# A graph kernel whose attention stage splits its weighted rows into bf16 parts in PSUM, on ScalarE and VectorE

## The chip, the cores and the metric

The kernel runs on one core of one Trainium2 chip. The metric is the device time of the whole kernel in microseconds, one launch from start to end.

## The reference

Four kinds of graph layer act on 6,250 nodes of 48 features, in eight layers, each with a residual and a norm. The change touches the second kind. With 206,250 sorted edges it weights the rows of the target node by the edge's softmax weight and sums them at the source node:

```python
seg_max = jax.ops.segment_max(logits, dst, num_segments=N)
ex = jnp.exp(logits - seg_max[dst])
...
seg_sum = jax.ops.segment_sum(ex, dst, num_segments=N)
```

In the kernel the edges stand in cells (a bucket of 128 source nodes by a bucket of 128 target nodes). A row is fetched by a one-hot matmul, multiplied by its edge's weight, and added at its node by another one-hot matmul. The fp32 rows go through TensorE exactly enough as three bf16 parts: the high part, the high part of what it leaves, and the rest.

## The kernel before

Between about 3000 and 5850 us of the span three kinds of work are interleaved over the places of one loop, `for q in range(PLACES)`. Every engine runs the same loop and takes its part of each place in the order in which the code stands; semaphores tie them together.

- **The gates** of a later layer, one quad of four edge tiles in each of the first 403 places: TensorE `hidden` (L1285, L1286), ScalarE `gates` (L1534, L1535, L1540, L1543), TensorE `gate` (L1295), VectorE `near_gates` (L2350, L2351), which runs one place later, then GpSimd's four indirect scatters (L925), here called the burst of that quad. SyncE loads the edge attributes.
- **The attention steps**, 273 groups of nine tiles (n), each in the place that `STEP_AT` names. 175 steps stand in the place right behind the step before, 78 skip one place, 20 skip two and 3 skip three. TensorE's `attend_take(n)` fetches the rows by 27 matmuls (L1377) into PSUM bank n % 2. VectorE's `attend_rows(n)` reduces (L2619) and multiplies the bank by the weights (L2626) into the fp32 buffer `row_part(n, 0)` in SBUF. In step n VectorE's `attend_step` first subtracts for group n-1 (L2634) and for group n-2 (L2638), two fp32 subtractions in SBUF; then come `attend_rows(n)`, `build_K` (L2599), `build_S` (L2589) and at times `collect`. `attend_give(n-3)` adds the rows by nine matmuls (L1406); its operand `uppers` picks every second bf16 of the fp32 buffer, which is the upper half of each number.
- **The counting of the cells**, three rounds in each step: `count_cells` on TensorE (L1418) into bank 5, `blocks_out` on ScalarE (L1633) out of it, and the next round only after that. Between the three L1633 ScalarE prepares the one-hot rows of step n+2 (`distance` L1603, `turn` L1613).

The buffers `part_slots` (four, in `meta_b`, `ring` and `VQ`) hold the split rows. The 25 last groups (`BEHIND`) have their subtractions on GpSimd behind its scatters; the change leaves them alone. Before the change `attend_take(n)` waits until the multiplication of group n-2 has read the bank (`s_msg`).

A step's row on TensorE is: take, count round 1, `hidden`, count round 2, `gate`, count round 3, give. In the profile `ps` is any PSUM bank, and `remote` as a releaser means a wait for which the profile names no work of this core.

## Time and profile before

| | us |
|---|---|
| median of 3 runs | 6898.89 |
| range of the runs | 6873.34 to 6902.73 |
| the profiled execution, device time | 6892.13 |
| its span | 6890.3 |
| TensorE busy | 3922.0 (57%) |
| VectorE busy | 4075.6 (59%) |
| ScalarE busy | 2567.7 (37%) |
| GpSimd busy | 3960.8 (57%) |

The busy times are over the whole span, whose stages have different limits; no engine is full overall. The stage with the attention steps takes over 40% of the span, and only there do instructions change. Times in the rows are in us from the span's start, and the mean of one instruction is in ns.

### The profile page before, as it was taken

The page shows a single profiled execution, that of the slowest core. Times are in us where ns is not written, and L with a number is a line of the kernel's source. Part 1 is how long each engine was busy: PE and PEld are TensorE (multiplying, and loading weights), DVE is VectorE, ACT ScalarE, POOL GpSimd, SP SyncE. Part 2 cuts the span into 40 slices and gives each one's busy share as a digit, 9 for nine tenths or more (in the row PEclk, how much of TensorE's full clock was granted, in tenths as well). Part 3 has the DMA queues.
Part 4 walks back from the last instruction along what each step waited for, and adds up shares of the span by engine and source line. Part 5 has one row for each costly group of instructions (what it writes and reads, how often), then busy time and mean ns, then how long its engine had stood idle before and what let it go on. Part 6 is the DMA issues. An engine that isn't in the chain of part 4 may idle for free.

```text
span 6890.3 us, 121918 instructions
## 1 busy us (share of the span) xinstructions
PE 3922.0 (57%) x46612; PEld 3008.3 (44%) x46613; DVE 4075.6 (59%) x7184; ACT 2567.7 (37%) x5259; POOL 3960.8 (57%) x3993
## 2 busy tenths in 40 slices
PE   5445555555555554345555555555555555887875
PEld 5344444323323333134444444444444444776774
DVE  4444443555555556345666666566666558667999
ACT  1111111111111111244455455445445445776664
POOL 2566666666666666655555555555555553225996
PEclk8555555555555555555555555555555556999998
DMA  3444311121111121123333233333333332667886
GB/s 127 167 160 161 124 49 47 48 55 49 47 49 47 48 49 47 32 50 54 58 56 57 56 58 55 56 56 58 55 58 56 55 56 54 189 189 172 193 191 130
DMA packets 1414672, 571.31 MB, mean 83 GB/s; under 512 B 1069539, under 2 KB 1353711, under 8 KB 1413953
## 3 DMA queue, kind: packets, MB, share of 16 engines
q1 hardware_dynamic: 1309185, 452.39, 29.3%
q0 software_dynamic: 104896, 110.96, 6.7%
q8 instruction: 381, 6.24, 0.4%
q14 instruction: 210, 1.72, 0.1%
HBM read 394.81 MB, written 168.16 MB: 82 GB/s over the span
## 4 chain that ended last, share of the span: by engine, by line
another core or an unknown queue 22%; PE 19%; issue 18%; ACT 15%; DVE 14%; DMA 9%; SPq 2%; POOL 1%; DVEq 0%; ACTq 0%; POOLq 0%
DMA rb<-dst_rows 5%; PE ps L1247 4%; ACT rb L1603 3%; DMA meta_b<-blocks 3%; ACT at_table L1633 3%; ACT meta_b L1613 2%; DVE ps L2096 2%; ACT meta_a L1535 2%; PE ps L1285 2%; PE ps L1418 2%; PE ps L1207 2%; ACT meta_b L1620 1%; PE ps L1235 1%; PE ps L1295 1%
## 5 line engine op out<-in xcount | busy, mean ns | idle before, releaser
L925 POOL DMA_INDIRECT by_src<-meta_a,row_src x1612 | 1613.9, 1001 | 1336.6 <-DVE meta_a L2351 916.7
L914 POOL DMA_INDIRECT ring<-h_table,meta_b x1616 | 1646.1, 1019 | 941.0 <-issue 449.7
L1520 ACT ACTIVATE ring<-ring,meta_b 128x48 f32<-128x48 f32 x1616 | 387.7, 325 | 2144.7 <-DMA ring<-h_table,meta_b 2076.2
L1418 PE MATMUL ps<-dst_i,meta_b 128*128 128x128 bf16 x2450 | 395.8, 293 | 907.9 <-ACT at_table L1633 641.1
L1633 ACT ACTIVATE at_table<-ps 128x384 uint8<-128x384 f32 x817 | 397.6, 487 | 1276.3 <-remote 1126.7
L1247 PE MATMUL ps<-ring,WX 128*128 128x48 bf16 x2188 | 438.7, 235 | 542.5 <-DVE row_src L2227 308.9
L2589 DVE TENSOR_TENSOR meta_b<-big,ps 128x1152 bf16<-128x1152 bf16 x546 | 734.7, 1346 | 0.0
L1418 PEld LDWEIGHTS ps<-dst_i,meta_b 128*128 128x128 bf16 x2450 | 229.2, 151 | 1137.2 <-issue 1107.4
L1247 PE MATMUL ps<-row_src,WX 128*128 128x48 bf16 x4376 | 494.5, 233 | 253.6 <-issue 252.5
L1377 PE MATMUL ps<-WX,meta_b 128*128 128x49 bf16 (+1 forms) x14742 | 588.9, 200 | 66.9 <-issue 36.4
L1247 PEld LDWEIGHTS ps<-ring,WX 128*128 128x128 bf16 x2188 | 360.2, 165 | 572.1 <-DVE row_src L2227 317.9
L1377 PEld LDWEIGHTS ps<-WX,meta_b 128*128 128x128 bf16 (+1 forms) x14742 | 569.9, 108 | 82.0 <-ACT meta_b L1620 40.3
L1285 PE MATMUL ps<-meta_a,w1T 40*48 40x256 f32 x806 | 399.9, 593 | 354.3 <-DMA meta_a<-in_attrT 194.0
L1247 PEld LDWEIGHTS ps<-row_src,WX 128*128 128x128 bf16 x4376 | 438.8, 167 | 281.4 <-issue 279.9
L2154 DVE TENSOR_SCALAR WX<-rb,place_c 128x1024 bf16<-128x1024 int16 x202 | 102.0, 505 | 687.2 <-remote 570.5
L1295 PE MATMUL ps<-w2T,meta_a 113*128 113x96 f32 x1612 | 435.7, 422 | 64.7 <-DVE meta_a L2351 38.7
L2350 DVE TENSOR_TENSOR meta_a<-ps,meta_a 128x192 f32<-128x192 f32 x403 | 142.9, 354 | 556.0 <-PE ps L1295 238.9
L1295 PEld LDWEIGHTS ps<-w2T,meta_a 113*128 113x128 f32 x1612 | 365.2, 313 | 186.2 <-issue 178.1
L1620 ACT ACTIVATE meta_b<-rb,steep_c 128x1152 fp8e4<-128x1152 uint8 x273 | 339.9, 1256 | 191.5 <-DMA rb<-dst_rows 185.5
L1286 PE MATMUL ps<-meta_a,w1T 40*48 40x256 f32 x806 | 402.7, 596 | 3.5 <-issue 3.4
L1235 PE MATMUL ps<-meta_a,WX 128*128 128x33 bf16 x6564 | 275.0, 192 | 224.5 <-issue 220.3
L1235 PEld LDWEIGHTS ps<-meta_a,WX 128*128 128x128 bf16 x6564 | 225.4, 107 | 333.9 <-issue 323.9
(342 smaller groups left out, 8836.7 us busy)
## 6 DMA issues: line engine op xcount, KB each, us to landing
meta_b<-blocks SPq DMA_DIRECT2D x490, 144.0 KB
by_src<-default SPq DMA_DIRECT2D x44, 1456.0 KB
meta_a<-by_src SPq DMA_DIRECT2D x273, 216.0 KB, 4.4
rb<-lo_rows SPq DMA_DIRECT2D x202, 256.0 KB
rb<-src_rows SPq DMA_DIRECT2D x273, 144.0 KB
rb<-dst_rows SPq DMA_DIRECT2D x273, 144.0 KB
blocks<-at_table SPq DMA_DIRECT2D x229, 144.0 KB
meta_a<-in_attrT SPq DMA_DIRECT2D x402, 80.0 KB
```

The source lines that it names most:

```text
L914: pool.indirect_dma_start(ring[:, gg % RING, j, 0:width], None, table, bass.IndirectOffsetOnAxis(ap=index(g * GROUP + j), axis=0)) \
L925: pool.indirect_dma_start(by_src, bass.IndirectOffsetOnAxis(ap=row_src[:, t:t + 1], axis=0), rec[:, q % RECS, j, :], None).then_inc(s_sc[q ...
L1235: mm = pe.matmul(bank(7, EJ, at=j * EJ), ohT_e[:, g % 2, h, j * P:(j + 1) * P], ej_p[:, at:at + EJ], start=(h == k == 0), stop=((h, k) == ...
L1247: mm = pe.matmul(acc_of(FROM[T] + h, FEAT), hot_w[:, g % 2, h, :, j], rows, start=False, stop=False, skip_group_check=True)
L1285: pe.matmul(bank(4, QH, FEAT), w1T[0:ATTR, :], attr[0:ATTR, c % 2, at:at + QH], start=True, stop=True)
L1286: pe.matmul(ps[HALF:HALF + FEAT, 4 * BANK:4 * BANK + QH], w1T[HALF:HALF + ATTR, :], attr[HALF:HALF + ATTR, c % 2, at:at + QH], start=True, ...
L1295: mm = pe.matmul(bank(6, 2 * FEAT, at=j * 2 * FEAT), sT[0:HALF + FEAT + 1, r % 2, j * P:(j + 1) * P], w2T[:, :], start=True, stop=True)
L1377: mm = pe.matmul(bank(m % 2, w, at=j * w), (ohT_8 if m >= SGROUPS else ohT_n)[:, m % 3, j * P:(j + 1) * P], XP[:, cell_dst(m % SGROUPS * S ...
L1418: mm = pe.matmul(bank(5, P, at=i * P), ohS_n[:, a % 3, :, u * TRIO + i], ohK_n[:, a % 2, u * TRIO + i, :], start=True, stop=True)
L1620: act.activation(ohT_8[:, m % 3, :], rb_8[:, m % 3, :], ACT.Abs_reciprocal_sqrt, bias=steep_c[:, 0:1], scale=STEEP, saturate=False) \
L1633: act.activation(blk_out[:, a % 3, u * TRIO * P:u * TRIO * P + w], bank(5, w), ACT.Copy).then_inc(s_blke, 1)
L2589: dve.tensor_tensor(ohS_n[:, m % 3, :, :], lo[:, n * SG:(n + 1) * SG][:, None, :].to_broadcast([P, P, SG]), place_ps[:, :, None].to_broadc ...
```

## The change

For the 248 groups that are not in `BEHIND` the multiplication writes its result back into its own PSUM bank. ScalarE copies the bank as bf16 into `third(n, 0)`; VectorE subtracts that part from the bank, in place; ScalarE copies the bank again as bf16 into `third(n, 1)`; VectorE subtracts once more and writes bf16 into `third(n, 2)`. The three parts now lie next to each other as bf16, and `attend_give` reads them without a stride. Two semaphores are new (`s_hi`, `s_mid`). `attend_take(n)` waits in addition for the last subtraction of group n-2 (`s_lop`), since the bank is in use until then.

```diff
+        s_hi, s_mid = s_hit[1], s_step[1]
...
+        def took(n):
+
+            return bank(n % 2, SG * EW).rearrange("p (j w) -> p j w", j=SG)
+
+        def third(n, i):
+
+            return part_slots[n % 4].bitcast(BF16)[:, 0:SG * PARTS * EW] \
+                .rearrange("p (j i w) -> p j i w", j=SG, i=PARTS)[:, :, i, :]
+
+        def thirds(n, j):
+
+            return part_slots[n % 4].bitcast(BF16)[:, j * PARTS * EW:(j + 1) * PARTS * EW]
...
                     if n >= 2:
                         pe.wait_ge(s_msg, n - 1)
+                        if n - 2 not in BEHIND:
+                            pe.wait_ge(s_lop, n - 1)
                     sum_parts(n, EW)
...
-                        mm = pe.matmul(bank(2 + d % 2, XW), ohS_n[:, n % 3, :, j], uppers(n, j, EW),
+                        mm = pe.matmul(bank(2 + d % 2, XW), ohS_n[:, n % 3, :, j],
+                                       uppers(n, j, EW) if n in BEHIND else thirds(n, j),
...
+                    parted = 0 <= n - 1 < SGROUPS and n - 1 not in BEHIND
+                    if parted:
+                        act.wait_ge(s_msg, n)
+                        if n - 1 >= 4:
+                            act.wait_ge(s_nr, n - 4)
+                        act.activation(third(n - 1, 0), took(n - 1), ACT.Copy).then_inc(s_hi, 1)
                     blocks_out(3 * (n - 3))
...
                     blocks_out(3 * (n - 3) + 2)
+                    if parted:
+                        act.wait_ge(s_rest, n)
+                        act.activation(third(n - 1, 1), took(n - 1), ACT.Copy).then_inc(s_mid, 1)
...
-                    if n >= 4:
+                    if n in BEHIND and n >= 4:
                         dve.wait_ge(s_nr, n - 3)
-                    dve.tensor_tensor(row_part(n, 0, EW), bank(n % 2, SG * EW).rearrange("p (j w) -> p j w", j=SG), by,
-                                      ALU.mult).then_inc(s_msg, 1)
+                    dve.tensor_tensor(row_part(n, 0, EW) if n in BEHIND else took(n), took(n), by, ALU.mult).then_inc(s_msg, 1)
...
-                    if 0 <= n - 1 < SGROUPS and n - 1 not in BEHIND:
-                        dve.wait_ge(s_msg, n)
-                        dve.tensor_tensor(row_part(n - 1, 1, EW), row_part(n - 1, 0, EW), upper(n - 1, 0, EW), ALU.subtract) \
-                            .then_inc(s_rest, 1)
-                    if 0 <= n - 2 < SGROUPS and n - 2 not in BEHIND:
-                        dve.wait_ge(s_rest, n - 1)
-                        dve.tensor_tensor(row_part(n - 2, 2, EW), row_part(n - 2, 1, EW), upper(n - 2, 1, EW), ALU.subtract) \
-                            .then_inc(s_lop, 1)
+                    parted = 0 <= n - 1 < SGROUPS and n - 1 not in BEHIND
+                    if parted:
+                        dve.wait_ge(s_hi, n)
+                        dve.tensor_tensor(took(n - 1), took(n - 1), third(n - 1, 0), ALU.subtract).then_inc(s_rest, 1)
                     if n < SGROUPS:
                         attend_rows(n)
                     if 0 <= n - 2 < SGROUPS:
                         build_K(n - 2)
                         build_S(n - 2)
+                    if parted:
+                        dve.wait_ge(s_mid, n)
+                        dve.tensor_tensor(third(n - 1, 2), took(n - 1), third(n - 1, 1), ALU.subtract).then_inc(s_lop, 1)
```

How the order on the engines changes is shown at one place in the middle of the stage. VectorE before, from the gates of a quad through one step to the next gates (`s_red` is the counting's semaphore, `s_mT` the take's, `s_diag` the give's, `s_prod` is `s_rest`):

```order
L2350 TENSOR_TENSOR meta_a<-ps,meta_a 128x4x48 [waits s_small,s_gp]
L2351 TENSOR_TENSOR meta_a<-meta_a,mj_t 128x4x48 [waits s_dve]
L2634 TENSOR_TENSOR VQ<-VQ 128x9x49 [waits s_msg]
L2638 TENSOR_TENSOR ring<-ring 128x9x49 [waits s_prod]
L2619 TENSOR_REDUCE big<-meta_b 128x9 [waits s_oha,s_rowc]
L2626 TENSOR_TENSOR meta_b<-ps,big 128x9x49 [waits s_diag,s_mT]
L2599 TENSOR_TENSOR dst_i<-at_table,ps 128x512 [waits s_red]
L2599 TENSOR_TENSOR dst_i<-at_table,ps 128x640
L2589 TENSOR_TENSOR meta_b<-big,ps 128x1152 [waits s_diag]
L2350 TENSOR_TENSOR meta_a<-ps,meta_a 128x4x48 [waits s_small,s_gp]
```

The same place after the change (line numbers of the new file; `s_hit1` is `s_hi`, `s_step1` is `s_mid`):

```order
L2376 TENSOR_TENSOR meta_a<-ps,meta_a 128x4x48 [waits s_small,s_gp]
L2377 TENSOR_TENSOR meta_a<-meta_a,mj_t 128x4x48 [waits s_dve]
L2660 TENSOR_TENSOR ps<-ps,VQ 128x441 [waits s_hit1]
L2645 TENSOR_REDUCE big<-meta_b 128x9 [waits s_oha,s_rowc]
L2652 TENSOR_TENSOR ps<-ps,big 128x441 [waits s_mT]
L2625 TENSOR_TENSOR dst_i<-at_table,ps 128x512 [waits s_red]
L2625 TENSOR_TENSOR dst_i<-at_table,ps 128x640
L2615 TENSOR_TENSOR meta_b<-big,ps 128x1152 [waits s_diag]
L2668 TENSOR_TENSOR VQ<-ps,VQ 128x9x49 [waits s_step1]
L2376 TENSOR_TENSOR meta_a<-ps,meta_a 128x4x48 [waits s_small,s_gp]
```

The second subtraction has moved from ahead of the reduction to the end of the step, ahead of the next gates, and serves the group of the step before. ScalarE before, one step and the gates behind it:

```order
L1633 ACTIVATE at_table<-ps 128x384 [waits s_h2w0,s_red]
L1603 ACTIVATE rb<-rb,place_c 128x1152 [waits s_rowd2]
L1633 ACTIVATE at_table<-ps 128x384 [waits s_red]
L1613 ACTIVATE meta_b<-rb,ones 128x1152 [waits s_abs,s_deg,s_mT]
L1633 ACTIVATE at_table<-ps 128x384 [waits s_red]
L1534 ACTIVATE meta_a<-ps,b1c 48x256 [waits s_gp,s_sp]
```

The same step after the change:

```order
L1662 ACTIVATE VQ<-ps 128x9x49 [waits s_diag,s_msg]
L1650 ACTIVATE at_table<-ps 128x384 [waits s_h2w0,s_red]
L1620 ACTIVATE rb<-rb,place_c 128x1152 [waits s_rowd2]
L1650 ACTIVATE at_table<-ps 128x384 [waits s_red]
L1630 ACTIVATE meta_b<-rb,ones 128x1152 [waits s_abs,s_deg,s_mT]
L1650 ACTIVATE at_table<-ps 128x384 [waits s_red]
L1672 ACTIVATE VQ<-ps 128x9x49 [waits s_prod]
L1551 ACTIVATE meta_a<-ps,b1c 48x256 [waits s_gp,s_sp]
```

One copy now stands ahead of the first block and one behind the third, ahead of the next gates. On TensorE the order stays; the first matmul of a take waits for one semaphore more.

## Rows read from the trace of the kernel before

**Rows 1.** Busy time by stretch: window, its length, each engine's busy us, PEclk, DMA share.

```profile
3000.00:5700.00 2700.00, 1544.47 (x13997) 1149.33 (x13993) 1665.23 (x2705) 1331.79 (x2715) 1457.93 (x1467) 0.56 0.32 56
```

**Rows 2.** The waits, 3000 to 5700 us: engine, tile and line, releaser: total, times, longest.

```profile
ACT at_table L1633 <- remote: 1124.5, 237, 15.8
POOL by_src L925 <- DVE meta_a L2351: 865.1, 242, 7.0
...
DVE meta_b L2626 <- remote: 278.8, 90, 9.9
```

**Rows 3.** Groups by line on VectorE, 3000 to 5700 us; the last, whole run.

```profile
L2589 DVE TENSOR_TENSOR meta_b<-big,ps 128x1152 bf16<-128x1152 bf16 x246 | 331.5, 1347 | 0.0
...
L2634 DVE TENSOR_TENSOR meta_b<-meta_b 128x441 f32<-128x441 f32 x123 | 75.3, 613 | 0.0
L2626 DVE TENSOR_TENSOR meta_b<-ps,big 128x441 f32<-128x441 f32 x122 | 75.3, 617 | 290.5 <-remote 278.8 <-issue 10.8
...
L2096 DVE TENSOR_TENSOR_SCAN ps<-ps,carry,zeros_b 128x403 f32<-128x403 f32 x147 | 155.5, 1058 | 267.1 <-remote 135.2 <-PE ps L1148 127.4 <-issue 4.4
```

**Rows 4.** The same on ScalarE and GpSimd; the last, ScalarE, whole run.

```profile
L1633 ACT ACTIVATE at_table<-ps 128x384 uint8<-128x384 f32 x735 | 357.8, 487 | 1232.8 <-remote 1124.5 <-PE ps L1418 65.6 <-issue 42.2
...
L925 POOL DMA_INDIRECT by_src<-meta_a,row_src x1467 | 1459.1, 995 | 1242.4 <-DVE meta_a L2351 865.1 <-issue 377.3
...
L1503 ACT ACTIVATE WX<-ps,rb 96x512 f32<-96x512 f32 x50 | 31.4, 679 | 160.7 <-PE ps L1066 96.8 <-remote 63.9
```

**Rows 5.** Timeline, one place right behind another: start us, us, engine, line, [idle].

```profile
4012.97 0.35 DVE L2350 TENSOR_TENSOR meta_a<-ps,meta_a 128x192 f32<-128x192 f32 x1
4013.01 0.49 ACT L1633 ACTIVATE at_table<-ps 128x384 uint8<-128x384 f32 x1
...
4013.53 1.33 PE L1377 MATMUL ps<-WX,meta_b 128*128 128x49 bf16 x27
...
4013.99 1.09 POOL L925 DMA_INDIRECT by_src<-meta_a,row_src  x1 [4.96 <-DVE meta_a L2351]
...
4016.92 0.49 ACT L1633 ACTIVATE at_table<-ps 128x384 uint8<-128x384 f32 x1 [2.26 <-remote]
...
4019.97 0.49 ACT L1633 ACTIVATE at_table<-ps 128x384 uint8<-128x384 f32 x1
...
4020.35 0.46 ACT L1534 ACTIVATE meta_a<-ps,b1c 48x256 f32<-48x256 f32 x1
...
4020.50 1.33 PE L1377 MATMUL ps<-WX,meta_b 128*128 128x49 bf16 x27
```

**Rows 6.** Timeline, a take behind and a take ahead of the scatters' start.

```profile
4004.11 1.10 POOL L925 DMA_INDIRECT by_src<-meta_a,row_src  x1 [2.36 <-DVE meta_a L2351]
...
4005.07 1.33 PE L1377 MATMUL ps<-WX,meta_b 128*128 128x49 bf16 x27
...
4009.96 0.49 ACT L1633 ACTIVATE at_table<-ps 128x384 uint8<-128x384 f32 x1 [3.76 <-remote]
...
4180.81 1.33 PE L1377 MATMUL ps<-WX,meta_b 128*128 128x49 bf16 x27
...
4181.59 1.10 POOL L925 DMA_INDIRECT by_src<-meta_a,row_src  x1 [5.77 <-DVE meta_a L2351]
...
4186.96 0.48 ACT L1633 ACTIVATE at_table<-ps 128x384 uint8<-128x384 f32 x1
```

**Rows 7.** Timeline, a take in the place after one without a step.

```profile
4715.01 1.09 POOL L925 DMA_INDIRECT by_src<-meta_a,row_src  x1 [6.63 <-DVE meta_a L2351]
...
4716.42 1.33 PE L1377 MATMUL ps<-WX,meta_b 128*128 128x49 bf16 x27
...
4726.76 0.49 ACT L1633 ACTIVATE at_table<-ps 128x384 uint8<-128x384 f32 x1 [1.33 <-remote]
```

**Rows 8.** Timeline: third L1633 of step 20 and of step 245.

```profile
3214.20 0.49 ACT L1633 ACTIVATE at_table<-ps 128x384 uint8<-128x384 f32 x1
...
5668.44 0.48 ACT L1633 ACTIVATE at_table<-ps 128x384 uint8<-128x384 f32 x1
```

## The prediction

> **What bounds the kernel now.** I read three views, in this order. The busy time by stretch first: from 3000 to 5700 us, where all changed instructions lie, VectorE is busy for 1665 of 2700 us, TensorE for 1544, GpSimd for 1458 and ScalarE for 1332 [rows 1]. Nobody is full, so engine time saved or added counts only where it lies on the loop of waits. The waits second: ScalarE stands 1124.5 us in front of `blocks_out`, released by "remote"; GpSimd stands 865.1 us until `near_gates` is done; VectorE's multiplication stands 278.8 us, in one of its three buffer forms, with "remote" again [rows 2]. Both "remote" waits begin behind a take: the multiplication and the counts queued behind the take are released late, though the take's own record lasts only 1.33 us. The timeline third, to see when they are late. In a usual place right behind another the take starts at 4013.53, the scatters of the gates at 4013.99, and the third block ends at 4020.46; the next take starts at 4020.50 [rows 5]. Where the take starts 0.96 us after the scatters, the first block is not released until 4.89 us after it; where it starts 0.78 us before them, the third block ends 6.6 us after the take's start [rows 6]. A take or count that runs beside a burst of scatters gets its results out late. What sets a step is thus the row take, count, block, three times, and how it lies to the burst.
>
> I measure a step from T, the end of its third block, to the next one's. Between the blocks of steps 20 and 245, of which the first and the last stand in [rows 8], lie 225 steps in 2454 us: 141 right behind another at 7.85 us each, 63 with one place between at 14.2, 18 with two at 20.7, 3 with three at 26.5. The take starts on average 0.10 us before T in the first kind, 2.99 us after T in the second. From the take's start to the third block's end it is 7.96 us in the first kind on average: 6.78 in the 10 places where the take starts 0.7 to 1.2 us before the burst, 7.44 in the 57 where it is 0.3 to 0.6 before, 8.73 in the 23 where it is 0.3 to 1.2 after. In the second kind it is 11.2; an example is 10.8, with the take 1.4 us after the burst's start [rows 7].
>
> **The change part by part.** It touches 248 steps: by the shares above and the places named ahead, about 157 right behind another, 70 with one place between, 21 with more.
>
> *VectorE's three operations.* Count and elements stay, 441 a piece. From PSUM into SBUF the multiplication takes 617 ns, between SBUF buffers the subtraction takes 613 [rows 3]. The source thus costs 4 ns. No row writes back into PSUM with this shape; the nearest that does is a scan over 403 elements at 1058 ns [rows 3], which bounds each of the three from above at 1.16 us, while 0.61 bounds them from below. I take 0.62, since it is the same operation. Beside the row: the Trainium skill ("VectorE: DVE Perf Modes", Rules for kernel authors) says to copy a matmul's output to SBUF first if many operations follow, which speaks against working in PSUM. The row shows 4 ns in 617, so by the trace it is worth nothing here.
>
> *ScalarE's two copies.* 441 elements from PSUM. Between 487 ns for 384 elements and 679 ns for 512 [rows 4] it is 0.57 us; these two rows are also its bounds. Together 248 x 2 x 0.57 = 283 us of work. The first copy stands ahead of the first block, where ScalarE waits anyway (2.26 us in the usual place [rows 5]); it costs nothing, and where that wait were gone it would cost 0.57 a step. The second follows the third block, and there nothing hides it.
>
> *TensorE's give* reads its parts without a stride. It runs behind the third count, beside the third block; in the rows the take follows the block's end by 0.04 us [rows 5], so a shorter give brings nothing.
>
> *The new wait, right behind another step.* Before, the take starts at T. After, it needs the last subtraction of group n-2, made at the end of step n-1. ScalarE can start an operation 0.1 us before T (4020.35 against 4020.46 [rows 5]), so the second copy ends at T + 0.47, the subtraction at T + 1.09, and with 0.15 for the release, an estimate, the take starts at T + 1.25. Queued behind the wait on TensorE are count 1, `hidden` and the rest of its row. On VectorE the next `near_gates` stands behind the same subtraction: it starts at T + 1.09, and the burst 1.02 us later (4012.97 to 4013.99 [rows 5]), at T + 2.1. Before, it started at T + 0.5. So the take now starts 0.85 us ahead of the burst. That is the position in which the rest takes 6.78 in place of the mean 7.96. The step becomes 1.25 + 6.78 = 8.03 against 7.85: +0.18 x 157 = +28 us.
>
> *With one place between.* The subtraction is long done when the take is due. But the copy pushes ScalarE's gates by 0.45, and with them `hidden` and the take, to T + 3.44. The burst starts at T + 2.1, and the take comes 1.3 after that, where 13 places (0.8 to 1.9 after) average 11.1; with 11.2 the step is 14.64 against 14.22: +0.42 x 70 = +30 us.
>
> *With more between.* The delay is between the copy's 0.45 and the full 1.35 of a take; I take the middle: +0.9 x 21 = +19 us.
>
> *Can VectorE keep up?* The first copy waits for ScalarE's second copy and the gates' four operations (some 1.3 us): it ends at T + 2.35. Then come subtraction, reduction, multiplication, two one-hot builds and the last subtraction: 0.62 + 1.35 + 0.62 + 1.35 + 1.35 + 0.62 = 5.9 (the three long ones are of 1152 elements like L2589, 1347 ns [rows 3]), to T + 8.27. From one last subtraction to the next that is 7.2 us, below 8.03. VectorE is close but does not set the step.
>
> **The sum.** 28 + 30 + 19 = +77 on the profiled execution's 6892, so 6969. That execution lies 7 us below the median of 6899, and I use its own time. If the operations in PSUM were at their upper bound, the step would be set by VectorE and gain 0.5 to 0.8 us each (+80 to +125 in the 157 steps); the copies' bounds make -20 to +27 over 248 steps. Forecast with its own range: 6860 to 7080.
>
> **The rivals.**
>
> *The early take brings no relief* (slower by much). The wait is paid, 1.35 x 157 + 0.45 x 91 = 253 us, and the rest of the place stays at 7.96: 7145. For it: only 10 places show the early position, and they may be early because they are light ones. Against it: the second place of [rows 6] has a full burst of scatters and all three blocks, and still 6.6. It decides from a rest of some 7.5 on. The Trainium skill ("SBUF — State Buffer", SBUF: two separate sides) says that TensorE's port waits for nobody and that only VectorE and GpSimd share one. By it the burst could not hold up a take at all, and this rival would stand. The trace speaks against it, 4.89 us against 3.39 to the first block between [rows 6] and [rows 5], without telling by which resource.
>
> *The burst is moved clear of take and blocks* (faster). Two places show 5.74 from the take to the third block. Then VectorE's 7.2 sets the step: -0.65 x 157 = -102, and with the same relief in the second kind -0.7 x 70 = -49: 6741. For it: the wait of ScalarE is 1124.5 us in all [rows 2], the greatest reserve, and small shifts of the burst move it by whole microseconds. Against it: the burst lasts some 5 us (four L925 of 995 ns [rows 4] and their gaps) and still covers the later counts.
>
> *Nothing shows* (the new wait is met by work that is late anyway, the copies hide): 6892, give or take 30. For it: in 23 of 141 places the step is paced by a late burst. Against it: in most, nothing stands between the block's end and the take but 0.04 us.
>
> **How the numbers follow.** Forecast 0.43, no relief 0.22, clear of the burst 0.25, nothing shows 0.10. A measurement of this kernel can tell 0.5% (34 us) from no change. Of the forecast's 0.43, 0.30 lies above that and 0.11 within, 0.02 below; no relief is all slower; clear of the burst all faster; nothing shows within. So faster 0.27, same 0.21, slower 0.52. The range takes in the forecast's own and reaches to each of the two far cases, leaving out about half of either: 6735 to 7140.
>
> **What would show it.** TensorE's take is released by VectorE's last subtraction, some 1.2 us after the third block, in places right behind another; ScalarE's two new lines at 0.57 us, VectorE's three at 0.62; bursts that start 0.85 us behind the takes; the "remote" wait of `blocks_out` down by about 1.2 us in each such place; steps right behind another at 8.03, with one place between at 14.6. I am wrong if operations on PSUM cost clearly more than 0.62, if VectorE has no idle time left in the step, or if the rest of the place is not shorter with an earlier take.

## The result and the profile after

The changed kernel takes 6951.77 us (median of 5 runs, 6948.9 to 6968.72), the kernel before 6900.88 (5 runs). The ratio is 1.009, 95% interval 1.0075 to 1.0106: 51 us between the medians, 62 by the ratio, and 77 were forecast. The profiled execution after took 6963.9 us, with a span of 6962.0.

The experiments ran on four chips, and the same kernel before took very different times on them. To compare them I call the levels A (6900 us, the result above), B (6796 us on the chip of e1 to e4, 6800 on that of b0, a0, e6 and e8) and C (5596 us on the chip of e9 to e11, 5593 on that of a1). All ratios are against the kernel before on the same chip. Why the chips differ so much is not known. The change itself was measured at all three: 1.009 at A, 0.9999 (0.9987 to 1.0012) at B, 1.017 (1.0153 to 1.0187) at C. So 0.9% is not the change's price, but its price at A; the experiments tell what it is made of.

The stage after, in the views of [rows 1] to [rows 4]. Busy time by stretch, with the columns of [rows 1]:

```profile
3000.00:5700.00 2700.00, 1588.68 (x13693) 1145.19 (x13695) 1644.37 (x2652) 1548.69 (x3144) 1390.15 (x1435) 0.51 0.32 55
```

The waits, as in [rows 2]; the last one is new:

```profile
POOL by_src L939 <- DVE meta_a L2377: 941.4, 239, 8.3
...
ACT at_table L1650 <- remote: 770.0, 184, 16.3
...
DVE ps L2652 <- remote: 338.0, 87, 14.4
...
DVE meta_b L2668 <- ACT meta_b L1672: 180.1, 71, 5.2
```

Groups by line, VectorE, ScalarE, GpSimd, TensorE:

```profile
L2652 DVE TENSOR_TENSOR ps<-ps,big 128x441 f32<-128x441 f32 x242 | 149.8, 619 | 361.8 <-remote 338.0 <-issue 23.6
...
L2668 DVE TENSOR_TENSOR meta_b<-ps,meta_b 128x441 bf16<-128x441 f32 x122 | 75.5, 619 | 195.6 <-ACT meta_b L1672 180.1 <-issue 15.5
L2660 DVE TENSOR_TENSOR ps<-ps,meta_b 128x441 f32<-128x441 f32 x121 | 75.4, 623 | 33.6 <-ACT meta_b L1662 18.4 <-issue 13.6
...
L1662 ACT ACTIVATE meta_b<-ps 128x441 bf16<-128x441 f32 x121 | 66.4, 549 | 3.0
L1672 ACT ACTIVATE meta_b<-ps 128x441 bf16<-128x441 f32 x121 | 66.1, 546 | 0.0
...
L939 POOL DMA_INDIRECT by_src<-meta_a,row_src x1435 | 1390.8, 969 | 1307.7 <-DVE meta_a L2377 941.4 <-issue 366.3
...
L1391 PE MATMUL ps<-WX,meta_b 128*128 128x49 bf16 x6507 | 311.5, 217 | 205.0 <-DVE meta_b L2668 95.2 <-DVE VQ L2668 45.8 <-DVE ring L2668 42.3
```

The new and moved instructions cost what was forecast: VectorE 619 and 623 ns, ScalarE 549 and 546 ns. The "remote" wait of `blocks_out` fell from 1124.5 to 770.0 us. The multiplication's fell too: it has one buffer form now, with 338.0 us, where the two forms that [rows 2] leaves out add 168.9 and 147.0 us to its 278.8, 594.7 in all:

```profile
DVE VQ L2626 <- remote: 168.9, 51, 9.1
DVE ring L2626 <- remote: 147.0, 47, 12.7
```

In their place stand new waits, TensorE's take for L2668 and VectorE's L2668 for the copy L1672 (180.1 us in one buffer form of three), and GpSimd's for its gates grew from 865.1 to 941.4 us.

The timeline of the same step as [rows 5], right behind another:

```profile
4044.11 0.49 ACT L1650 ACTIVATE at_table<-ps 128x384 uint8<-128x384 f32 x1
4044.48 0.55 ACT L1672 ACTIVATE meta_b<-ps 128x441 bf16<-128x441 f32 x1
...
4045.06 0.62 DVE L2668 TENSOR_TENSOR meta_b<-ps,meta_b 128x441 bf16<-128x441 f32 x1 [0.25 <-issue]
...
4045.59 0.35 DVE L2376 TENSOR_TENSOR meta_a<-ps,meta_a 128x192 f32<-128x192 f32 x1
...
4045.83 1.29 PE L1391 MATMUL ps<-WX,meta_b 128*128 128x49 bf16 x27 [0.99 <-DVE meta_b L2668]
...
4046.61 0.97 POOL L939 DMA_INDIRECT by_src<-meta_a,row_src  x1 [2.12 <-DVE meta_a L2377]
...
4048.00 0.49 ACT L1650 ACTIVATE at_table<-ps 128x384 uint8<-128x384 f32 x1 [1.25 <-PE ps L1435]
...
4051.05 0.49 ACT L1650 ACTIVATE at_table<-ps 128x384 uint8<-128x384 f32 x1
```

The third block ends at 4044.60, the copy at 4045.03, the last subtraction at 4045.68, and the take starts at 4045.83: 1.23 us behind the block (forecast 1.25). The gates' product starts at 4045.59, the burst at 4046.61, 0.78 us behind the take's start (forecast 0.85). The first block is released 2.17 us after the take's start, where it was 3.39 in [rows 5]; on average over the 141 steps of this kind it is 2.23 us, and was 4.13.

All steps between the blocks of steps 20 and 245, measured from third block to third block as in the prediction (means in us over 141 steps right behind another, 63 with one place between, 18 with two):

| kernel, level | ratio to before | right behind | one between | two between | block to take | take to third block |
|---|---|---|---|---|---|---|
| before, A | 1 | 7.85 | 14.22 | 20.68 | -0.10 | 7.96 |
| changed, A | 1.009 | 7.60 | 15.02 | 22.35 | 1.33 | 6.26 |
| before, B | 1 | 7.71 | 13.63 | 20.31 | -0.13 | 7.84 |
| changed, B | 0.9999 | 7.25 | 14.29 | 21.91 | 1.34 | 5.90 |
| e1, B | 1.0411 | 9.03 | 14.73 | 21.03 | 1.38 | 7.64 |
| e2, B | 0.9916 | 7.00 | 14.60 | 20.89 | -0.22 | 7.22 |
| e3, B | 0.9960 | 7.50 | 13.88 | 20.51 | 0.00 | 7.50 |
| e4, B | 1.0017 | 7.28 | 14.45 | 21.63 | -0.09 | 7.37 |
| e6, B | 0.9978 | 7.17 | 14.59 | 20.83 | 1.36 | 5.80 |
| e8, B | 0.9912 | 6.96 | 14.62 | 20.84 | -0.27 | 7.23 |
| changed, C | 1.0170 | 6.94 | 9.45 | 13.09 | 1.45 | 5.49 |
| e9, C | 1.0440 | 7.65 | 10.11 | 12.76 | 2.44 | 5.21 |
| e10, C | 1.0327 | 6.96 | 10.62 | 13.57 | -0.01 | 6.98 |
| e11, C | 1.0013 | 6.15 | 9.27 | 14.03 | -0.09 | 6.24 |

The last two columns are those of the steps right behind another. The rows "before, B" and "changed, B" are b0 and a0, from another chip than e1 to e4. There is no profile of the kernel before at C; "changed, C" is a1. At A the stage got 51 us longer between those two blocks: -0.25 x 141 = -35, +0.80 x 63 = +51, +1.67 x 18 = +30, and +6 for the three longest steps. The other 20 us between the two profiled executions lie outside it, 13 of them ahead of the stage's first take, where no code changed.

### The profile page after: what moved, and what is told of

It reads as the page before. It is cut to its first block, busy times and chain, and to the rows that moved or that the text cites. A ratio compares the mean times of both kernels' runs of the same rounds, so it can differ in the third digit from the quotient of the medians.

```text
span 6962.0 us, 122414 instructions
## 1 busy us (share of the span) xinstructions
PE 4010.0 (58%) x46612; PEld 3029.9 (44%) x46613; DVE 4091.5 (59%) x7184; ACT 2815.6 (40%) x5755; POOL 3920.1 (56%) x3993
## 3 DMA queue, kind: packets, MB, share of 16 engines
q8 instruction: 381, 6.24, 0.4%
## 4 chain that ended last, share of the span: by engine, by line
PE 20%; another core or an unknown queue 20%; issue 17%; DVE 16%; ACT 14%; DMA 9%; SPq 2%; POOL 2%; DVEq 0%; ACTq 0%; POOLq 0%
DMA rb<-dst_rows 5%; PE ps L1261 4%; DMA meta_b<-blocks 3%; ACT rb L1620 2%; PE ps L1299 2%; ACT meta_b L1630 2%; PE ps L1435 2%; DVE ps L2122 2%; ACT at_table L1650 2%; PE ps L1391 2%; PE ps L1221 2%; ACT meta_b L1637 1%; ACT meta_a L1552 1%; PE ps L1249 1%
## 5 line engine op out<-in xcount | busy, mean ns | idle before, releaser
L939 POOL DMA_INDIRECT by_src<-meta_a,row_src x1612 | 1575.4, 977 | 1433.4 <-DVE meta_a L2377 1017.4
L1435 PE MATMUL ps<-dst_i,meta_b 128*128 128x128 bf16 x2450 | 411.4, 304 | 723.4 <-ACT at_table L1650 420.4
L1391 PE MATMUL ps<-WX,meta_b 128*128 128x49 bf16 (+1 forms) x14742 | 586.7, 201 | 261.4 <-DVE meta_b L2668 97.5
L1391 PEld LDWEIGHTS ps<-WX,meta_b 128*128 128x128 bf16 (+1 forms) x14742 | 555.7, 108 | 317.6 <-issue 259.8
L1299 PE MATMUL ps<-meta_a,w1T 40*48 40x256 f32 x806 | 432.0, 637 | 323.1 <-ACT meta_a L1552 158.5
L1309 PE MATMUL ps<-w2T,meta_a 113*128 113x96 f32 x1612 | 454.4, 437 | 72.7 <-DVE meta_a L2377 46.7
L1309 PEld LDWEIGHTS ps<-w2T,meta_a 113*128 113x128 f32 x1612 | 383.7, 328 | 196.0 <-issue 174.5
L1300 PE MATMUL ps<-meta_a,w1T 40*48 40x256 f32 x806 | 434.0, 640 | 0.1
L2652 DVE TENSOR_TENSOR ps<-ps,big 128x441 f32<-128x441 f32 x248 | 153.5, 619 | 372.9 <-remote 349.2
L2625 DVE TENSOR_TENSOR dst_i<-at_table,ps 128x1152 bf16<-128x1152 f32 (+8 forms) x316 | 368.8, 1178 | 0.3 <-PE ps L1435 0.3
```

The costliest lines, as they stand in the source:

```text
L939: pool.indirect_dma_start(by_src, bass.IndirectOffsetOnAxis(ap=row_src[:, t:t + 1], axis=0), rec[:, q % RECS, j, :], None).then_inc(s_sc[q ...
L1299: pe.matmul(bank(4, QH, FEAT), w1T[0:ATTR, :], attr[0:ATTR, c % 2, at:at + QH], start=True, stop=True)
L1300: pe.matmul(ps[HALF:HALF + FEAT, 4 * BANK:4 * BANK + QH], w1T[HALF:HALF + ATTR, :], attr[HALF:HALF + ATTR, c % 2, at:at + QH], start=True, ...
L1309: mm = pe.matmul(bank(6, 2 * FEAT, at=j * 2 * FEAT), sT[0:HALF + FEAT + 1, r % 2, j * P:(j + 1) * P], w2T[:, :], start=True, stop=True)
L1391: mm = pe.matmul(bank(m % 2, w, at=j * w), (ohT_8 if m >= SGROUPS else ohT_n)[:, m % 3, j * P:(j + 1) * P], XP[:, cell_dst(m % SGROUPS * S ...
L1435: mm = pe.matmul(bank(5, P, at=i * P), ohS_n[:, a % 3, :, u * TRIO + i], ohK_n[:, a % 2, u * TRIO + i, :], start=True, stop=True)
```

## The experiments

### Is it the position to the burst? (e1, e2)

e1 is the changed kernel with one thing moved on VectorE:

```diff
                     if 0 <= q - 1 < QUADS_IN:
                         near_gates(q - 1)
+                    for n in steps_at(q - 1):
+                        if 0 <= n - 1 < SGROUPS and n - 1 not in BEHIND:
+                            last_part(n)
                     for n in steps_at(q):
                         attend_step(n)
```

`last_part(n)` is the last subtraction, which no longer stands at the end of `attend_step`.

> The changed kernel, but VectorE multiplies the gates of the quad (near_gates) ahead of the last subtraction of the step before, not behind it. Theory P (position): the rest of a place, from the take's start to the third block's end, depends on how the take lies to the burst of scatters. Here the burst starts about 0.7 us earlier and the take 0.2 us later, so the take falls at or behind the burst's start; the rest goes from 6.3 back to 8 or 9 us in places right behind another, the step from 7.6 to 9.5 or more, and the time to 7150 to 7300 us. Rival X (ports): the rest became short because VectorE no longer reads two SBUF buffers in its subtractions; position is indifferent, the rest stays 6.3 and the time 6940 to 6990 us.

Measured at B: 1.0411 (1.0365 to 1.0457), where the changed kernel has 0.9999. The wait ahead of the take is the same (1.38 against 1.34), the rest went from 5.90 to 7.64 us. The same step as above in e1's timeline:

```profile
4059.00 0.49 ACT L1650 ACTIVATE at_table<-ps 128x384 uint8<-128x384 f32 x1
...
4059.98 0.97 POOL L939 DMA_INDIRECT by_src<-meta_a,row_src  x1 [4.99 <-DVE meta_a L2377]
...
4060.72 1.29 PE L1391 MATMUL ps<-WX,meta_b 128*128 128x49 bf16 x27 [0.99 <-DVE meta_b L2656]
...
4064.23 0.49 ACT L1650 ACTIVATE at_table<-ps 128x384 uint8<-128x384 f32 x1 [2.58 <-remote]
...
4067.28 0.49 ACT L1650 ACTIVATE at_table<-ps 128x384 uint8<-128x384 f32 x1
```

The third block ends at 4059.49, the burst starts at 4059.98, the take at 4060.72, and its first block comes 3.51 us later. In the median the burst starts 0.74 us ahead of the take, where it was 0.79 behind it. The split in PSUM is all there, only the burst is ahead of the take, and the relief is gone. The loss is smaller than expected (a rest of 8 to 9 us, a step of 9.5 or more): the rest is 7.64, a little under the 7.84 of the kernel before at B, and the step 9.03. The rival by ports, which asked for 6940 to 6990 us, falls.

e2 is the kernel before with `near_gates` behind the two subtractions:

```diff
-                    if 0 <= q - 1 < QUADS_IN:
+                    if 0 <= q - 1 < QUADS_IN and not steps_at(q):
                         near_gates(q - 1)
...
                             .then_inc(s_lop, 1)
+                    if 0 <= q - 1 < QUADS_IN:
+                        near_gates(q - 1)
                     if n < SGROUPS:
                         attend_rows(n)
```

> The kernel before, with near_gates moved behind the two subtractions in places with a step; nothing else, so no new wait, no copies, all parts in SBUF. P: the burst starts 1.2 us later, 1.7 us behind the take, the rest falls to 5.2 to 5.5 us, the step right behind another to VectorE's 6.6 to 6.8; 6700 to 6800 us. X: the subtractions still read two SBUF buffers, the rest stays at 8 us: 6890 to 6960 us.

Measured at B: 0.9916 (0.9893 to 0.994), a gain of 59 us with nothing but the order, where 100 to 200 were expected. The rest fell to 7.22 us and not to 5.2 to 5.5, the step to 7.00 and not to 6.6 to 6.8. A step in its timeline:

```profile
3902.79 0.49 ACT L1633 ACTIVATE at_table<-ps 128x384 uint8<-128x384 f32 x1
...
3903.32 1.33 PE L1377 MATMUL ps<-WX,meta_b 128*128 128x49 bf16 x27
...
3904.83 0.97 POOL L925 DMA_INDIRECT by_src<-meta_a,row_src  x1 [6.57 <-DVE meta_a L2351]
...
3905.00 0.49 ACT L1633 ACTIVATE at_table<-ps 128x384 uint8<-128x384 f32 x1 [0.56 <-PE ps L1418]
...
3908.05 0.49 ACT L1633 ACTIVATE at_table<-ps 128x384 uint8<-128x384 f32 x1
```

The take starts 1.51 us ahead of the burst, the first block comes 1.68 us after it and the step takes 5.26 us from block to block. In the 63 steps right behind another whose take lies more than 0.8 us ahead of a burst the mean of the rest is 6.2 us. But such steps are nearly as short as a burst with its gaps (5.1 us), so the bursts are pushed into the places behind: in 24 others the take falls 3.5 to 5 us into one, and the rest is 7.5. And the steps with one place between grew from 13.63 to 14.60. The position rule holds at B; that all steps can have the good position at once doesn't.

### What do PSUM and the copies cost? (e3, e4)

e3 keeps the parts in SBUF and takes only the change's order and wait:

```diff
                         if n >= 2:
                             pe.wait_ge(s_msg, n - 1)
+                        if n - 2 not in BEHIND:
+                            pe.wait_ge(s_lop, n - 1)
...
-                    if 0 <= n - 2 < SGROUPS and n - 2 not in BEHIND:
-                        dve.wait_ge(s_rest, n - 1)
-                        dve.tensor_tensor(row_part(n - 2, 2, EW), row_part(n - 2, 1, EW), upper(n - 2, 1, EW), ALU.subtract) \
-                            .then_inc(s_lop, 1)
...
                         build_K(n - 2)
                         build_S(n - 2)
+                    if 0 <= n - 1 < SGROUPS and n - 1 not in BEHIND:
+                        dve.wait_ge(s_rest, n)
+                        dve.tensor_tensor(row_part(n - 1, 2, EW), row_part(n - 1, 1, EW), upper(n - 1, 1, EW), ALU.subtract) \
+                            .then_inc(s_lop, 1)
```

> The kernel before with only the order and the wait of the change: the last subtraction at the end of the step after its group's, ahead of the next gates, and the take waits for it; the parts stay fp32 in SBUF and ScalarE copies nothing. P: without the copy to wait for, the take starts 0.2 to 0.4 us behind the third block and 0.8 ahead of the burst; the step right behind another 6.6 to 7.0 us, 6730 to 6830 us in all. X: rest 8 us as before, take 0.3 later: 6930 us. The difference to the changed kernel is what PSUM and the two copies cost.

Measured at B: 0.9960 (0.9939 to 0.9981). The take does not wait at all (0.00 us): without a copy the last subtraction is done when the third block ends. With it the gates come earlier than expected, and only a part of the takes gets the good position: 44 of the 141 start 0.6 to 0.8 us ahead of a burst, with a rest of 6.3 us, and 23 further ahead, with 6.1; 33 start 0.3 to 1.2 us into one, with 8.1, and 9 fall 7 us and more into a row of bursts, with 11.9. The mean rest is 7.50. The expectation erred in the position and so in the size, 7.50 us a step and not 6.6 to 7.0; the rival's sign, slower than before, is wrong as well. The copies and PSUM on top cost 0.4% at B, by the ratios of two chips: they win 0.25 us in a step right behind another and lose 0.41 with one place between and 1.40 with two.

e4 is the changed kernel with the second copy earlier:

```diff
                     blocks_out(3 * (n - 3) + 1)
+                    if parted:
+                        act.wait_ge(s_rest, n)
+                        act.activation(third(n - 1, 1), took(n - 1), ACT.Copy).then_inc(s_mid, 1)
                     if n + 2 < SGROUPS:
                         turn(n + 2)
                     blocks_out(3 * (n - 3) + 2)
-                    if parted:
-                        act.wait_ge(s_rest, n)
-                        act.activation(third(n - 1, 1), took(n - 1), ACT.Copy).then_inc(s_mid, 1)
```

> The changed kernel with ScalarE's second copy ahead of turn and the third block, no longer behind it. P: the take starts 0.7 us after the third block in place of 1.3, as far ahead of the burst as before (0.8), and where no step follows ScalarE's gates are not held up by 0.55; the copy may delay the third block by up to 0.55. Step right behind another 7.0 to 7.5 us, one place between 14.5: 6820 to 6900 us. If ScalarE's row sets the step instead, the copy only changes its place: 6940 to 6960 us.

Measured at B: 1.0017 (0.9995 to 1.0039), no better than the change at the same level (0.9999). The wait ahead of the take is gone (-0.09 us against 1.34) and nothing is gained: the rest grew from 5.90 to 7.37. One step in the timeline; L1669 is the copy in its new place:

```profile
4005.68 0.49 ACT L1650 ACTIVATE at_table<-ps 128x384 uint8<-128x384 f32 x1
...
4006.35 1.09 PE L1391 MATMUL ps<-WX,meta_b 128*128 128x49 bf16 x27 [0.35 <-DVE meta_b L2668]
...
4007.35 0.55 ACT L1662 ACTIVATE ring<-ps 128x441 bf16<-128x441 f32 x1
...
4007.79 0.48 ACT L1650 ACTIVATE at_table<-ps 128x384 uint8<-128x384 f32 x1
...
4009.67 0.56 ACT L1669 ACTIVATE ring<-ps 128x441 bf16<-128x441 f32 x1
...
4011.24 0.51 ACT L1650 ACTIVATE at_table<-ps 128x384 uint8<-128x384 f32 x1
```

The take starts early, the first block comes at 4007.79 behind the gates and the first copy L1662, and from it to the third one the copy L1669 adds its 0.56. ScalarE is never idle in this step, which ends at 4011.75, 5.58 us after the one before it (4006.17). So a single step can be far shorter than the 7.25 of the changed kernel. But such steps bring the bursts of scatters together: in 15 of the 141 (2 in the changed kernel at B) the take falls 7 to 10 us into a row of bursts, and there the rest is 12.3. The time is the expectation's second answer, its reason, ScalarE's row, only a part: 0.56 of the 1.47.

### Why did the steps with places between lose? (e6, e8)

b0 and a0 are the kernels before and after once more, as the base at B:

> The kernel before itself, for a profile from the same chip as the three other runs of this call: steps right behind another near 7.8 us, with one place between 14.2, with two 20.7.

> The changed kernel itself, on the chip of this call: 0.7 to 1.1% over the kernel before, steps right behind another 7.6 us, with one place between 15.0, with two 22.3.

b0 took 6799.37 us, one run; a0 0.9999 of the kernel before, not the 1.007 to 1.011 expected. All three kinds of steps are shorter than at A, and the steps right behind another gain more (-0.46 in place of -0.25 us).

e6 moves both new operations, ScalarE's second copy and VectorE's last subtraction, behind the gates where no step follows; elsewhere they stay at the end of `attend_step`:

```diff
                         gates(q, True)
+                    for n in steps_at(q - 1) if not steps_at(q) else []:
+                        if 0 <= n - 1 < SGROUPS and n - 1 not in BEHIND:
+                            second_part(n)
...
                         near_gates(q - 1)
+                    for n in steps_at(q - 1) if not steps_at(q) else []:
+                        if 0 <= n - 1 < SGROUPS and n - 1 not in BEHIND:
+                            last_part(n)
```

> The changed kernel, but where the next place has no step ScalarE's second copy goes behind the next gates and VectorE's last subtraction behind the next near_gates; where a step follows at once all stays. Theory G: the loss of 0.8 us with one place between and 1.7 with two comes from these two operations standing ahead of the gates. Then these steps go back to 14.2 to 14.5 and 20.7 to 21.0 us, the steps right behind another stay at 7.6, and the time falls by 60 to 85 us against the changed kernel, to 0.3% under the kernel before or level with it. Rival: the loss comes from the longer chain of the split (the take that waits, TensorE's lower clock); then these steps stay at 15.0 and the time at 0.9% over before.

Measured at B: 0.9978 (0.9963 to 0.9994), 0.2% or 14 us under the changed kernel, not 60 to 85. Theory G is right with two places between (21.91 back to 20.83) and wrong with one (14.29, now 14.59). There the loss has another place. The copy ahead of the gates does cost what was forecast: the take starts 3.07 us behind the block before, 3.62 with the change, 3.17 in e6 (all at B). But the rest is 11.43 in e6, against 10.67 with the change and 10.56 before. In the trace at A the first block of such a step comes sooner after the take than before (6.04 us on average against 6.94), but from the first to the third block it takes 5.36 against 4.30. A step of this kind after the change, the one of [rows 7]:

```profile
4765.94 1.09 POOL L939 DMA_INDIRECT by_src<-meta_a,row_src  x1 [6.79 <-DVE meta_a L2377]
...
4766.74 1.33 PE L1391 MATMUL ps<-WX,meta_b 128*128 128x49 bf16 x27
...
4770.98 0.49 ACT L1650 ACTIVATE at_table<-ps 128x384 uint8<-128x384 f32 x1 [3.74 <-remote]
4771.14 0.96 POOL L939 DMA_INDIRECT by_src<-meta_a,row_src  x1 [0.30 <-issue]
...
4774.57 0.49 ACT L1650 ACTIVATE at_table<-ps 128x384 uint8<-128x384 f32 x1 [1.96 <-remote]
...
4774.96 0.96 POOL L939 DMA_INDIRECT by_src<-meta_a,row_src  x1 [0.30 <-issue]
...
4777.45 0.49 ACT L1650 ACTIVATE at_table<-ps 128x384 uint8<-128x384 f32 x1 [1.25 <-remote]
```

Rounds 2 and 3 of the counting run beside the burst of the second quad (from 4771.14), and ScalarE stands in front of each. The bursts now start later behind a step, and so reach further into the next. e6 shows the other side at B: with the two operations behind the gates, first to third block takes 4.62 us again (4.51 before, 5.71 with the change), but the first block comes 6.81 us after the take (6.05 before, 4.96 with the change). The first round loses more than the other two win. That is read from the traces; no run here isolates it. The rival of the expectation, TensorE's lower clock, isn't excluded: e6's stage has the changed kernel's granted clock (0.51, 0.56 before), its `hidden` product takes 634 ns (593 before), and its steps with one place between stayed long.

e8 tries to keep e2's gain without its loss; its edit is shown against e2:

```diff
-                    if 0 <= q - 1 < QUADS_IN and not steps_at(q):
+                    if 0 <= q - 1 < QUADS_IN and not (steps_at(q) and steps_at(q - 1)):
                         near_gates(q - 1)
...
-                    if 0 <= q - 1 < QUADS_IN:
+                    if 0 <= q - 1 < QUADS_IN and steps_at(q - 1):
                         near_gates(q - 1)
```

> The kernel before with near_gates behind the two subtractions only in places right behind a step. Theory P (position) with G: the steps right behind another stay at the 7.0 us or less that they had with all gates behind, and the steps with a place between, which had 14.6 there, go back to 14.2 or less: 1.2 to 1.8% under the kernel before. If the two kinds are tied (bursts pushed out of the one land in the other) it is only the 0.8% seen with all gates behind.

Measured at B: 0.9912 (0.9884 to 0.9941), the same as e2, and the steps with one place between stay at 14.62 though their own order is that of before; their first block comes 7.38 us after the take, where it was 6.05. The kinds are tied: a burst that is put off in one place is in the way in the next. e2 and e8 are faster than both kernels at B; at A and C they were not tried.

### Is there slack in VectorE's row? (e9, e10, e11)

e9 and e10 do the reduction twice in the 248 steps, in the changed kernel and in the one before:

```diff
+                        if n not in BEHIND:
+                            dve.tensor_reduce(cell_of[:, (n + 8) * SG:(n + 9) * SG],
+                                              ohT_n[:, n % 3, :].rearrange("p (j n) -> p j n", n=P), AX_X, ALU.add)
                         dve.tensor_reduce(cell_of[:, n * SG:(n + 1) * SG],
```

> The changed kernel with VectorE's reduction ahead of the multiplication done a second time (into cells that are written over later) in the 248 steps of the change, 1.35 us each. Theory V: with the short rest, VectorE's own row, with its waits for the two copies, sets the steps right behind another; each of these 157 pays 0.9 to 1.35 us, the others little: 140 to 240 us over the changed kernel, 2 to 3.5% over the kernel before. Rival (as predicted at first): the step stands 0.5 to 0.8 us above VectorE's row, and pays only 0.6 us: about 90 us, 1.3%.

> The kernel before with the same second reduction. Theory V: VectorE's multiplication waits there 1.3 to 1.5 us for a take that is late, and the reduction goes into that wait: 0 to 60 us over the kernel before, less than half of what the same work costs the changed kernel. Rival: VectorE sets the steps in both kernels alike: 140 us and more in both.

Both ran at C: e9 1.044 (1.0422 to 1.0457), e10 1.0327 (1.031 to 1.0344). With the change itself at 1.017 there, the reduction costs the changed kernel 2.7% (5839.8 - 5690.7 = 149 us, 0.60 a step) and the kernel before 3.3% (183 us, 0.74 a step). e9 by itself falls where theory V put it (140 to 240 us over the changed kernel) and far above its rival's 90. But e10's is its rival's answer, 140 us and more in both kernels, and theory V, little for the kernel before, is wrong at C. There nothing is released late, so the wait that was to swallow the reduction doesn't exist. Whether it exists at A and B remains open. Of the 1.35 us that VectorE has to do more in each step, 0.6 to 0.75 show: about half goes into time in which the stage was not waiting for VectorE.

e11 puts `near_gates` between the two subtractions, in SBUF and without a new wait: the last subtraction as in e3, `near_gates` as in e2.

> The kernel before (parts in SBUF, no wait added) with near_gates behind the first subtraction and the second subtraction at the end of the step: the burst starts about 1.1 us behind the take's start. P: near the best position for a place right behind another without pushing the bursts into the next places as far as with near_gates behind both: steps 6.6 to 7.0 and, with one place between, 13.6 to 14.2 us: 1.0 to 1.6% under the kernel before, ahead of the 0.9% reached so far. If VectorE's row and the bursts' own length bound all these orders alike, it gives 0.9% again.

Measured at C: 1.0013 (1.0004 to 1.0023), so no gain. In the steps right behind another the place of the take doesn't matter at C: sorted by its distance to the nearest burst, their rest is 6.0 to 6.5 us in e11 and 5.2 to 5.8 in the changed kernel in every class with more than three steps, where at A it ran from 8.7 to 5.3. The waits on `blocks_out` at C, first e11 (2500 to 4300 us), then the changed kernel (2500 to 4500 us), where the stage is:

```profile
ACT at_table L1633 <- PE ps L1418: 300.4, 237, 7.1
```

```profile
ACT at_table L1650 <- PE ps L1435: 315.9, 289, 6.4
...
POOL by_src L939 <- DVE meta_a L2377: 171.4, 108, 4.9
```

No wait for "remote" stands near the top of either, where at A it was the first. The busy time of the same length of the stage in e11 and in the changed kernel:

```profile
2500.00:4300.00 1800.00, 1299.84 (x13052) 983.39 (x13049) 1531.84 (x2524) 1242.21 (x2537) 1382.90 (x1369) 0.65 0.45 79
```

```profile
2500.00:4300.00 1800.00, 1358.84 (x12410) 1007.09 (x12410) 1472.93 (x2403) 1392.24 (x2848) 1277.48 (x1314) 0.55 0.43 75
```

VectorE does 85% of 1800 us in e11 and 82% with the change; in steps right behind another its idle time is 0.03 us in the median in e11 and 0.43 in the changed kernel. So in e11 its row sets these steps, and the change makes it wait for ScalarE's copies there. But it doesn't bound e11's stage. GpSimd does. Its waits, first in e11 (2500 to 4300 us), then in the changed kernel (2500 to 4500 us, where it also stands the 171.4 us above for its gates):

```profile
POOL by_src L925 <- issue: 413.1, 1355, 0.3
```

```profile
POOL by_src L939 <- issue: 411.7, 1350, 0.3
```

In e11 the 1369 scatters (1011 ns each) and the gaps of 0.3 us between them fill the whole window (1382.9 + 413.1 of 1800 us). In the stage every burst starts 0.30 us behind the end of the one before it, and some 27 us behind its own gates, and the 333 places between steps 20 and 245 take 5.27 us each, a burst of 4.96 and its gap. No order on VectorE could have made this stage shorter, so e11 doesn't say what its order is worth where GpSimd has time left. In the changed kernel a place takes 5.58 us: in the same 1800 us GpSimd stands 151 us for its gates, and its 1314 scatters are 39 ns shorter (972 ns), 51 us in all. An estimate from these two, 151 - 51 = 100 us, is close to what the change costs at C (5690.7 - 5593.3 = 97 us). That the kernel before is bound by its scatters at C like e11 is likely from the time that they share, but there is no profile of it.

### The change where nothing is late (a1)

> The changed kernel itself once more. What it costs should depend on how late takes and counts are released beside the bursts on the chip at hand. Where the kernel before takes 6900 us (late): 0.9% over it; where 6800 us: level; where 5600 us (no late release, VectorE's row sets the steps): the wait is paid and brings nothing back, 0.8 to 1.6% over the kernel before, steps right behind another 6.0 us before and 6.6 to 6.8 after. A cost that is the same on every chip would speak against the explanation by lateness.

This run was at C again: 1.017, 0.1% more than the most that was expected, with steps of 6.94 us and not 6.6 to 6.8. The expected 6.0 us before can't be compared, for want of a profile; e11 has 6.15. The bound that the expectation named, VectorE's row, is right only for the steps right behind another. The wait ahead of the take is as at A and B (1.45), and the rest is 5.49. The cost differs with the chip in the order expected for C against the others. Between A and B it doesn't follow so simply: B is a little less late than A (from 3000 to 5500 us `blocks_out` waits 987 us for "remote" before the change, against 1026), and the change does better there.

## Why the prediction was right, and where its steps were not

- **What bounds the kernel** (nobody full, the row of take, counts and blocks, and its place beside the burst): right, shown at B by e1, where moving the burst takes the relief away, and by e2, where moving it gives relief. But it holds for the chips at A and B. At C, by e11, GpSimd's scatters bound the stage and VectorE's row the steps right behind another.
- **VectorE in PSUM** at 0.62 us, bounds 0.61 to 1.16: 0.619 and 0.623. Writing back into PSUM thus costs 2 ns on the multiplication (617 before) and 10 on the first subtraction (613 before). **ScalarE's copies** at 0.57: 0.55.
- **The new wait**: forecast 1.25 us behind the block, on average 1.33; the burst 0.85 us behind the take, 0.7 to 0.8 in 104 of the 141 steps.
- **The rest right behind another**: forecast 6.78, measured 6.26. The step became 7.60, not 8.03: it gained 0.25 us where a loss of 0.18 was forecast. The term +28 us should have been -0.25 x 157 = -39: here the forecast had the sign wrong, by the size of the relief. The mean of ten places before was too high an estimate; in the 104 it is 6.48, and in the 35 with more distance 5.3.
- **One place between**: forecast +0.42, measured +0.80, so the term +30 should have been +56. Half of the miss is the take, which came 3.62 us behind the block and not 3.44. e6 shows at B that the copy costs the 0.45 that was forecast (3.62 against 3.17), and that 0.10 is left without it (3.07 before). A term that the sum put at nothing is TensorE's slower clock: the four `hidden` products of a quad take 637 to 639 ns after the change and 589 to 591 before, by an estimate 0.19 us together; no run isolates it. The other half is the rest, 11.41 and not 11.2. Here only the take was placed against a burst, not rounds 2 and 3 of the counting against the second one, where by the traces the time went.
- **More between**: forecast +0.9, measured +1.67 and +2.0, so the term +19 should have been about +36. e6 shows at B that 1.1 of it (21.91 to 20.83) is the two operations ahead of the gates.
- **The rivals**: "no relief" is refuted by the rest of 6.26. "Clear of the burst" came true in 35 of the 141 steps, with a rest of 5.3, and not in the others. "Nothing shows" describes B, by two terms that cancel (-0.46 x 141 = -65, +0.66 x 63 + 1.6 x 18 = +70), not by its mechanism.

So the total came out near (77 against 51 to 62) because one term was put too high by 67 us and two too low by 43: the direction and the costs of the operations were forecast, the closeness of the total is luck. Had the chip been another one, the same argument would have met 0.0% or 1.7%.

## What to carry to other kernels

When a wait is added in front of one engine, look at what else it moves: here the subtraction stood ahead of GpSimd's gates, and moving the burst of scatters by 1.5 us gave back, in steps right behind another at A and B, what the wait of 1.3 us took. Place every operation of the row against the burst, not only the first, and for the places without a step too. The same order could be had without the wait, by moving two lines (e2, 0.8% faster than before at B), so ask of a gain which of the change's parts it belongs to. Look whether the engine that is to be moved out of the way has time left at all: in e11 the scatters ran without a pause, and no order could gain. And measure on more than one chip before a result under 2% is called one.

## What the runs showed of the hardware

- The same kernel takes 6900, 6796 and 5596 us on different chips. At A and B waits for takes and counts end late beside GpSimd's indirect DMAs (1124.5 us of "remote" on `blocks_out` at A); at C they don't, and there e11's stage goes at the pace of the scatters, 1.31 us each with their gap. What is late there is not settled: no run separates the resource.
- The scatters got shorter with the change: L925 at 995 ns, L939 at 969. Over the whole run it is 977 to 980 in the kernels with the subtractions in PSUM (changed, e1, e4, e6, e9) and 986 to 1015 in those with them in SBUF (before, e2, e3, e8, e10, e11). The Trainium skill ("SBUF — State Buffer", SBUF: two separate sides) says that a VectorE operation with two SBUF inputs and a GpSimd operation that reads SBUF exclude each other on a shared pair of ports. The trace agrees in sign, with 26 ns in 995, too little to matter at A; that this is the reason was not isolated.
- TensorE's granted clock over the stage fell from 0.56 to 0.51 at A, and L1285's 589 ns became 637 in its new line L1299; what is new on TensorE is that it stands still ahead of each take (205 us of idle time in front of L1391). For elementwise work on a matmul's output the Trainium skill ("VectorE: DVE Perf Modes", Rules for kernel authors) leaves the choice to accept the PSUM source or to copy to SBUF first if many operations follow. A subtraction took 610 to 613 ns between SBUF buffers and 619 to 623 on PSUM, 6 to 13 ns more at this size.
